# A sparse FFN cut into one-batch units and interleaved with the attention loops, its gate by tanh

## The chip, the cores and the metric

One Trainium2 chip, one core. The metric is the device time in microseconds of one execution of the whole program; lower is better. The profile is one execution, recorded by the hardware profiler. VectorE stands as DVE in it, ScalarE as ACT, GpSimd as POOL, TensorE as PE (its weight loads as PEld).

## What is computed

Two decoder layers on `x` of 4 batches x 256 tokens x 256 columns, f32, each an attention against a context and an FFN, both added to `x` with a gate `tanh(g)`. Layer 0: a retention-like attention with two heads, and a mixture of eight experts, of which each token takes one. Layer 1, where the change lies:

```
a  = grouped attention(layernorm(x), ctx), 32 heads in 8 groups, causal, softmax
x  = x + tanh(g_xattn[1]) * (a @ w_o.T + b_o)
y  = layernorm(x)
h  = silu(y @ w_gate) * (y @ w_up)          # 1024 columns
h  = of each four neighbouring columns only the two of largest magnitude, the others 0
x  = x + tanh(g_ffn[1]) * (h @ w_down)
```

## The kernel before, in words

The program is written by hand, one instruction stream for each engine, tied by semaphores; an engine runs its stream in order, and an instruction that waits holds all behind it. Tokens lie in 8 tiles of 128 (two a batch). The first 160 us are layer 0, the sort of tokens to experts and their loads; neither text nor change go there.

**The attention of layer 1.** For each batch `b` there are 24 score fills (`scores`, line 394, then the causal mask added by a bf16 matmul, line 410), each a PSUM bank of 512 columns, from which DVE takes row maxima (`row_maxima`, line 1151). The negated maxima (`negate`, lines 1161 and 1163) are turned by PE (`neg_turn`) and moved by DMA into rows of `qst`, so that a second product, `weights` (line 420), comes out with the maximum subtracted; ACT takes its exponential (`exponentials`, line 875), again 24 fills a batch. POOL zeroes the causal part (`affine_select`, line 730), eight times a batch. `values` (line 428) then makes four fills, ACT copies them out (`value_turn`), and twelve `finish` steps (per tile: four turns with DVE's reciprocal and product, one turn of the result, one projection by `wo1`, whose residual and statistics DVE makes) end the batch.

The order is the loop `for b in range(BATCH): for n in range(24)`, which every engine has in its own stream: in step `n` of batch `b` stand `weights(b, n)` and, while `n + 12 < 24`, `scores(b + 1, n + 12)` (LEAD is 12), then one `finish(b - 1, n // 2)` every second step, and the queries of batch `b + 2` at fixed steps. Behind the 24 steps come the keys of `b + 2` and the four `values(b, i)`, with three score fills of batch `b + 2` behind each.

PSUM has eight banks, dealt out in turn by `acquire` (line 191) from lists by kind: `max` 0 to 2 for scores, `exp` 3 to 5 for weights, `wide` 0 to 5 for values and the FFN, `turn1` 6 and `tok1` 7 for the rest. A fill waits until what stood in its bank is taken.

**The FFN of layer 1** stands behind all four batches, in two units of 512 tokens. `gate_up(g, j)` fills a bank with 512 gate columns and one with 512 up columns (two matmuls each); ACT takes silu of the first (line 931), DVE multiplies (line 1280), ACT takes the magnitude (line 925). Four such tiles `j`, in which neighbouring columns stand apart, make a group `g`. `sparsify(g, step)` (line 1233) finds the two largest of four: step 0 three compares (f32 in, bf16 out, lines 1241 to 1245), step 1 seven sums of them in bf16 (lines 1250 to 1263), steps 2 and 3 the masked products (line 1271). It runs one group behind. The first unit's gate steps carry the `finish` steps of batch 3 and the layer 3 norms of tiles 4 to 7 (the norms of tiles 0 to 3 stand in the loop of batch 3). `down(k)` is eight matmuls of 256 columns; `residual("res3", k, 3)` (line 986) ends a tile, which SP stores.

## Time and profile before

| | |
|---|---|
| three runs | 410.42 us median (410.26 to 411.62) |
| span of the profiled execution | 407.7 us; the page gives no time for it beside the span |
| busy: PE, DVE, ACT, POOL | 342.2, 214.7, 159.8, 98.1 us |
| mean granted TensorE clock | 0.937 |
| attention loops of batches 1, 2, 3 begin | at 222.2, 259.8, 286.2 us |
| values of batch 3 end, FFN begins | 309.0 us |
| last matmul ends | 405.1 us |

Of the page, the busy shares tell which engine could be the bound, and the chain which it is. A window is one stretch of the span: an engine whose busy time is nearly its length is what bounds it there, but a matmul's end is modelled, so PE can look busy while it waits; the pace of a stretch without waits shows its real speed. The granted clock is a share of 2.4 GHz.

### The profile page before, as it was taken

Reading aid. Unit: us, or ns where it says so; the run is one execution under the profiler, and the core shown is the slowest. Engines: PE = TensorE matmul, PEld = TensorE weight load, DVE = VectorE, ACT = ScalarE, POOL = GpSimd, SP = SyncE. Lnnn points to the kernel's source line nnn. Section 1 sums busy time; section 2 is a strip of 40 time slices with the busy share of each in tenths; the row PEclk is TensorE's granted clock in tenths of the full one; section 3 lists DMA queues with packets and bytes.
Section 4 is the critical chain, followed back from the end, with each engine's and each line's share of the span. In section 5 each row is a group of like instructions: output and inputs, shape, how many; then the busy total and the mean of one; then the engine's idle time right before and its main releaser. Section 6 shows DMA issues by size and latency. Waiting matters only on the chain.

```text
span 407.7 us, 4559 instructions
## 1 busy us (share of the span) xinstructions
PE 342.2 (84%) x1471; PEld 205.9 (50%) x1477; DVE 214.7 (53%) x509; ACT 159.8 (39%) x336; POOL 98.1 (24%) x148
## 2 busy tenths in 40 slices
PE   2799775509999848989799989979889879999997
PEld 1385565405656526545454555444443434444886
DVE  1544885601222248879446934881241338679921
ACT  1443221204333123145873875477873223333000
POOL 4402553330000256301340442054450001000000
PEclk9999998558999666999999999998999999999999
DMA  7995000134111115400000000000000000000011
GB/s 234 365 426 105 1 13 2 40 124 146 41 51 53 39 47 175 191 6 0 9 0 2 0 6 2 0 2 8 0 2 0 2 0 0 0 0 2 13 51 39
DMA packets 13879, 22.40 MB, mean 55 GB/s; under 512 B 2033, under 2 KB 11249, under 8 KB 13042
## 3 DMA queue, kind: packets, MB, share of 16 engines
q1 hardware_dynamic: 13090, 20.03, 14.5%
q0 software_dynamic: 768, 2.10, 1.6%
q8 instruction: 12, 0.20, 0.2%
q14 instruction: 9, 0.07, 0.1%
HBM read 15.83 MB, written 6.03 MB: 54 GB/s over the span
## 4 chain that ended last, share of the span: by engine, by line
PE 57%; DVE 20%; ACT 8%; issue 7%; DMA 3%; POOL 3%; another core or an unknown queue 1%; SPq 0%; DVEq 0%; ACTq 0%; POOLq 0%
PE bank L229 43%; DVE mx L1151 9%; PE bank L439 5%; ACT region L875 5%; PE bank L407 3%; DVE stats L946 2%; POOL x_sorted L692 2%; PE bank L242 1%; DMA ctxT<-in_ctxT_dram 1%; DVE x_sb L986 1%; PE bank L410 1%; PE bank L236 1%; PE bank L453 1%; PE bank L487 1%; ACT xT L747 1%
## 5 line engine op out<-in xcount | busy, mean ns | idle before, releaser
L1151 DVE TENSOR_REDUCE mx<-bank 128x2 f32<-128x512 f32 (+1 forms) x96 | 59.8, 684 | 14.0 <-PE bank L410 7.8
L875 ACT ACTIVATE region<-bank,padcol 128x512 f32<-128x512 f32 x96 | 60.8, 701 | 12.6 <-PE bank L229 11.6
L730 POOL TENSOR_SCALAR_AFFINE_SELECT region<-region 128x1024 f32<-128x1024 f32 x32 | 35.0, 1094 | 94.6 <-ACT region L875 94.3
L229 PE MATMUL bank<-xT,e_gu 128*128 128x512 f32 x128 | 56.6, 594 | 0.5 <-ACT xT L747 0.5
L229 PE MATMUL bank<-qst,kblk 128*128 128x512 f32 x96 | 46.1, 507 | 1.6 <-ACT region L875 0.7
L407 PE MATMUL bank<-kblk,qst 128*128 128x512 f32 x96 | 43.4, 475 | 1.7 <-DVE mx L1151 0.9
L229 PEld LDWEIGHTS bank<-xT,e_gu 128*128 128x128 f32 x128 | 23.8, 190 | 28.0 <-issue 27.1
L664 POOL TENSOR_SCALAR veps<-mv 128x1 f32<-128x1 f32 x40 | 11.3, 284 | 80.8 <-DVE mv L948 80.5
L410 PE MATMUL bank<-causb,identb 128*128 128x256 bf16 (+1 forms) x90 | 28.3, 314 | 0.0
L229 PE MATMUL bank<-e_down,region 128*128 128x256 f32 x128 | 27.8, 379 | 0.0
L986 DVE SCALAR_TENSOR_TENSOR x_sb<-bank,tg,x_sb 128x256 f32<-128x256 f32 x24 | 11.6, 482 | 29.2 <-PE bank L229 28.9
L747 ACT ACTIVATE xT<-bank 128x256 f32<-128x256 f32 x32 | 12.2, 386 | 37.5 <-PE bank L236 37.4
L229 PEld LDWEIGHTS bank<-e_down,region 128*128 128x128 f32 x128 | 24.3, 190 | 3.7 <-issue 0.5
L407 PEld LDWEIGHTS bank<-kblk,qst 128*128 128x128 f32 x96 | 18.3, 191 | 13.2 <-DVE mx L1151 9.3
L668 POOL TENSOR_TENSOR rstd<-veps,power 128x1 f32<-128x1 f32 x40 | 24.0, 601 | 3.3
L1123 DVE TENSOR_TENSOR sact<-bank,silu 128x176 f32<-128x176 f32 x15 | 5.1, 342 | 37.3 <-ACT silu L841 37.3
L1280 DVE TENSOR_TENSOR region<-bank,silu 128x512 f32<-128x512 f32 x16 | 11.0, 689 | 26.0 <-PE bank L229 26.0
L229 PEld LDWEIGHTS bank<-qst,kblk 128*128 128x128 f32 x96 | 18.7, 200 | 9.1 <-ACT region L875 7.3
L931 ACT ACTIVATE silu<-bank 128x512 f32<-128x512 f32 x16 | 9.6, 597 | 33.5 <-PE bank L229 33.5
L439 PE MATMUL bank<-region,vaug 128*32 128x512 f32 x192 | 22.7, 597 | 0.0
L229 PE MATMUL bank<-e_gu,sT 128*128 x60 | 21.7, 486 | 0.3 <-ACT sT L835 0.3
L229 PE MATMUL bank<-e_down,sT 128*128 (+1 forms) x60 | 19.6, 426 | 1.4 <-ACT sT L856 1.4
(155 smaller groups left out, 546.6 us busy)
## 6 DMA issues: line engine op xcount, KB each, us to landing
e_gu<-in_e_gu_dram SPq DMA_DIRECT2D x2, 1408.0 KB, 12.4
x_sorted<-zero SPq DMA_DIRECT2D x1, 1920.0 KB, 9.9
y_sorted<-region SPq DMA_DIRECT2D x15, 128.0 KB, 1.7
x_sb<-in_x_dram SPq DMA_DIRECT2D x4, 256.0 KB, 6.1
ctxT<-in_ctxT_dram SPq DMA_DIRECT2D x2, 512.0 KB, 6.1
e_down<-in_e_down_dram SPq DMA_DIRECT2D x1, 1024.0 KB, 14.3
region<-x_sorted SPq DMA_DIRECT2D x1, 1024.0 KB, 7.3
e_gu<-in_f_gate_dram SPq DMA_DIRECT2D x1, 1024.0 KB, 4.8
```

The lines of the kernel that those rows point to most:

```text
L229: return pe.matmul(dst, lhsT, rhs, start=first, stop=last)
L407: pe.matmul(dst, qst[:, s, q, hg, tile_cols(nt)], kblk[s][q][:, quads, 0:(nt + 1) * P], start=True, stop=False, skip_group_check=True)
L410: ready(pe.matmul(diagonal, identb[:, :], causb[:, 0:diagonal.shape[1], :], start=False, stop=True, skip_group_check=True), "sa")
L439: ins = pe.matmul(dst[32 * j:32 * j + 32, :], vaug[:, 2 * b + mt, 4 * q + j, :], rhs, start=(mt == 0), stop=(mt == nt), skip_group_check=True)
L664: pool.tensor_scalar(veps[:, layer, k:k + 1], mv[:, layer, k, 1:2], eps, None, ALU.add)\
L668: pool.tensor_tensor(out=rstd[:, layer, k:k + 1], in0=veps[:, layer, k:k + 1], in1=power[:, :], op=ALU.pow).then_inc(sem(f"rstd{layer}"), 1)
L730: pool.affine_select(out=block, in_=block, compare_op=ALU.is_ge, fill=0.0, base=0, pattern=[[0, 2], [0, PER_GROUP], [1, P]], channel_multi ...
L747: taken(act.activation(xT[:, :, tile_cols(tile)], src[:, 0:DIM].rearrange("p (t n) -> p t n", t=KT), ACT.Copy), f"ln{layer}")
L875: taken(act.activation(dst, src.rearrange("p (h n) -> p h n", n=SEQ - mt * P), ACT.Exp, bias=padcol[:, key:key + 1], scale=float(HD) ** -0 ...
L986: dve.scalar_tensor_tensor(out=x_sb[:, tile, :], in0=filled(dve, stage, k)[:, 0:DIM], scalar=tg[:, g:g + 1], in1=x_sb[:, tile, :], op0=ALU ...
L1151: taken(dve.reduce_max(mx[:, b % 2, nt, quads, q, hg], src, AX), "sa")
L1280: taken(dve.tensor_tensor(out=hs[u][:, 4 * blk + j, :], in0=src, in1=silu[:, i % 2, :], op=ALU.mult), "fu")
```

## The change

The FFN becomes four units of one batch (256 tokens). A bank now holds 256 gate and 256 up columns. A unit is 24 half steps: 0 to 15 are gate and up of its eight tiles in turn (two matmuls of 256 columns), 16 to 23 are down, two matmuls each: 16 to 19 the first group for both tiles, 20 to 23 the second. `ffn_halves` lays unit `b - 1` behind the steps from 16 of loop `b`, and its rest (half steps 8 to 23) behind steps 0 to 15 of loop `b + 1`; in the last loop two half steps a step. Each engine's loop calls its part (`ffn_half`, `ffn_gate`, `ffn_product`) at the end of the step. In the loops silu(g) is 0.5 * g * (1 + tanh(g / 2)), tanh on ACT and two DVE passes; the last unit keeps silu. The buffers `hs`, `absh`, the compares and counts are one group of half width; `hs` is two groups, each reused by the next unit. The banks: `max` and `exp` have two instead of three, `ffn` gets 4 and 5, values go to `exp`. `finish` takes steps 0 to 11, one each; queries, negation turn and norms move; the norms of layer 3 now stand in each loop. POOL makes their inverse deviations between its selects. The mask row is spread over four partitions for room, with wider loads and copies.

```diff
-QUERIES_AT = 10
-
-NORM_STEPS, LATE_NORM_STEPS = (13, 15, 17, 19), (3, 4, 6, 7)
-NEGATE_AT = 15
+QUERIES_AT = 13
+
+NORM_STEPS = (10, 15)
+NEGATE_AT = 18
+FFN_STEP = 16
+FFN_SLOTS = 2 * FFN_MT
+def ffn_halves(b, n):
+
+    if n < FFN_STEP:
+        return ((b - 2, 24 - FFN_STEP + n),) if b >= 2 else ()
+    if b == BATCH - 1:
+        return (b - 1, 2 * (n - FFN_STEP)), (b - 1, 2 * (n - FFN_STEP) + 1)
+    return ((b - 1, n - FFN_STEP),) if b >= 1 else ()
...
-        hs = [region[:, u, 0:4096].rearrange("p (m n) -> p m n", m=FFN_MT) for u in range(2)]
-        absh = [region[:, u, 4096:6144].rearrange("p (j n) -> p j n", j=4) for u in range(2)]
+        hs = (f_flat[:, 2 * KT * FFN_I:2 * KT * FFN_I + 4 * SEQ].rearrange("p (j n) -> p j n", j=4),
+              sT[:, :, :, :].rearrange("p s t n -> p (s t n)").rearrange("p (j n) -> p j n", j=4))
+        absh = sb("absh", [P, 4, SEQ])
+        xn3 = silu[:, :, SEQ:2 * SEQ]
...
-                 "max": (0, 1, 2), "exp": (3, 4, 5), "wide": (0, 1, 2, 3, 4, 5),
-                 "turn1": (6,), "tok1": (7,), "last": (6, 7)}
+                 "max": (0, 1), "exp": (2, 3), "ffn": (4, 5), "wide": (0, 1, 4, 5),
+                 "turn1": (6,), "tok1": (7,), "late": (6, 0, 1), "last": (0, 1, 2, 3, 4, 5)}
...
-                dst = acquire(pe, "av", 4 * b + i, "wide")
+                dst = acquire(pe, "av", 4 * b + i, "exp")
...
+            def ffn_half(b, h, kind="ffn"):
+
+                step, half = divmod(h, 2)
+                if step < FFN_MT:
+                    blk, j = divmod(step, 4)
+                    if half == 0:
+                        dst = acquire(pe, "ff", FFN_MT * b + step, kind)
+                    else:
+                        dst = fills["ff", FFN_MT * b + step]
+                    if h == 0:
+                        pe.wait_ge(sem("ln3_taken"), 2 * b + 2)
+                        if b == 0:
+                            loaded(pe, "f", 3)
+                    c = j * 2 * P + blk * P
+                    w = (f_gate, f_up)[half]
+                    for t in range(KT):
+                        ins = mm(dst[:, half * SEQ:(half + 1) * SEQ], w[:, t, c:c + P],
+                                 xT[:, t, b * SEQ:(b + 1) * SEQ], t == 0, t == KT - 1)
+                    if half == 1:
+                        ready(ins, "ff")
+                    return
+                blk, tile = divmod(step - FFN_MT, 2)
+                k = 2 * b + tile
+                if blk == 0 and half == 0:
+                    dst = acquire(pe, "res3", k, kind)[:, 0:DIM]
+                else:
+                    dst = fills["res3", k][:, 0:DIM]
+                pe.wait_ge(sem("hs_made"), FFN_MT * b + 4 * blk + 4)
+                for j in (2 * half, 2 * half + 1):
+                    m = 4 * blk + j
+                    ins = mm(dst, hs[blk][:, j, tile_cols(tile)], f_down[:, m, :], m == 0, m == FFN_MT - 1)
+                if blk == 1 and half == 1:
+                    ready(ins, "res3")
...
-                    if b >= 1 and n % 2 == 1:
-                        finish(b - 1, n // 2)
+                    if b >= 1 and n < 12:
+                        finish(b - 1, n)
                     if b + 2 < BATCH:
                         queries(b + 2, n)
-                    if b == BATCH - 1 and n in NORM_STEPS:
-                        ln_turn(3, NORM_STEPS.index(n), "tok1")
+                    if b >= 1 and n in NORM_STEPS:
+                        ln_turn(3, 2 * b - 2 + NORM_STEPS.index(n), "tok1")
                     if n == NEGATE_AT and b + 1 < BATCH:
                         neg_turn(b + 1, "turn1")
+                    for u, h in ffn_halves(b, n):
+                        ffn_half(u, h)
...
...
+            last = BATCH - 1
+            for n in (0, 1, 2, 3, 6, 7, 8, 9, 4):
+                finish(last, n, "late")
+            ffn_half(last - 1, 16)
+            finish(last, 10, "late")
+            finish(last, 5)
+            ffn_half(last - 1, 17)
+            finish(last, 11)
+            ffn_half(last - 1, 18)
+            ffn_half(last - 1, 19)
+            ln_turn(3, TILES - 2, "turn1")
+            ffn_half(last - 1, 20)
+            ffn_half(last - 1, 21)
+            ln_turn(3, TILES - 1, "tok1")
+            ffn_half(last - 1, 22)
+            ffn_half(last - 1, 23)
+            for h in range(24):
+                ffn_half(last, h, "last")
...
+                        if b >= 1 and q == 0 and n == 2:
+                            inverse_std(3, 2 * b - 2, LN_EPS)
+                        if b >= 1 and q == 1 and n == 0:
+                            inverse_std(3, 2 * b - 1, LN_EPS)
...
+            def magnitude(i):
+                g, j = divmod(i, 4)
+                act.wait_ge(sem("ff_taken"), i + 1)
+                if g >= 1 and j == 0:
+                    act.wait_ge(sem("compared"), 3 * g)
+                act.activation(absh[:, j, :], hs[g % 2][:, j, :], ACT.Abs).then_inc(sem("abs_made"), 1)
+
+            def ffn_gate(b, h):
+
+                step, half = divmod(h, 2)
+                if half == 0 or step > FFN_MT:
+                    return
+                i = FFN_MT * b + step
+                if step < FFN_MT:
+                    src = filled(act, "ff", i)[:, 0:SEQ]
+                    if i >= 2:
+                        act.wait_ge(sem("ff_taken"), i - 1)
+                    if b == BATCH - 1:
+                        act.activation(silu[:, i % 2, 0:SEQ], src, ACT.Silu).then_inc(sem("gate_made"), 1)
+                    else:
+                        act.activation(silu[:, i % 2, 0:SEQ], src, ACT.Tanh, scale=0.5).then_inc(sem("gate_made"), 1)
+                if step >= 1:
+                    magnitude(i - 1)
...

+            def ffn_product(b, h):
+
+                step, half = divmod(h, 2)
+                if half == 0:
+                    return
+                if step < FFN_MT:
+                    i = FFN_MT * b + step
+                    blk, j = divmod(step, 4)
+                    if b >= 1 and j == 0:
+                        dve.wait_ge(sem("res3_ready"), 2 * b)
+                    src = filled(dve, "ff", i)
+                    gate = silu[:, i % 2, 0:SEQ]
+                    dve.wait_ge(sem("gate_made"), i + 1)
+                    if b == BATCH - 1:
+                        taken(dve.tensor_tensor(out=hs[blk][:, j, :], in0=src[:, SEQ:2 * SEQ], in1=gate, op=ALU.mult), "ff")
+                    else:
+
+                        dve.scalar_tensor_tensor(out=gate, in0=gate, scalar=1.0, in1=src[:, 0:SEQ],
+                                                 op0=ALU.add, op1=ALU.mult).then_inc(sem("gated"), 1)
+                        dve.wait_ge(sem("gated"), i + 1)
+                        taken(dve.scalar_tensor_tensor(out=hs[blk][:, j, :], in0=gate, scalar=0.5, in1=src[:, SEQ:2 * SEQ],
+                                                       op0=ALU.mult, op1=ALU.mult), "ff")
+                    if blk == 1:
+                        sparsify(2 * b, j)
+                elif step < FFN_MT + 2:
+                    for part in (2 * (step - FFN_MT), 2 * (step - FFN_MT) + 1):
+                        sparsify(2 * b + 1, part)
+                else:
+                    residual("res3", 2 * b + step - FFN_MT - 2, 3)
...
-                    if b >= 1 and n % 2 == 1:
-                        finish(b - 1, n // 2)
+                    if b >= 1 and n < 12:
+                        finish(b - 1, n)
                     if b + 2 < BATCH:
                         queries(b + 2, n)
-                    if b == BATCH - 1 and n + 2 in NORM_STEPS:
-                        norm(3, NORM_STEPS.index(n + 2))
+                    if b >= 1 and n + 1 in NORM_STEPS:
+                        norm(3, 2 * b - 2 + NORM_STEPS.index(n + 1))
+                    for u, h in ffn_halves(b, n):
+                        ffn_product(u, h)
...
+            for n in (0, 1, 2, 3, 6, 7, 8, 9):
+                finish(last, n)
+            finish(last, 5)
+            ffn_product(last - 1, 17)
+            finish(last, 11)
+            norm(3, TILES - 2)
+            ffn_product(last - 1, 19)
+            norm(3, TILES - 1)
+            ffn_product(last - 1, 21)
+            ffn_product(last - 1, 23)
+            for h in range(24):
+                ffn_product(last, h)
```

`sparsify` is the function of before on one shared group of buffers, 256 columns wide.

## Rows read from the trace of the kernel before

**Rows 1.** The page: busy time of the engines, and the chain by engine.
```profile
PE 342.2 (84%) x1471; PEld 205.9 (50%) x1477; DVE 214.7 (53%) x509; ACT 159.8 (39%) x336; POOL 98.1 (24%) x148
PE 57%; DVE 20%; ACT 8%; issue 7%; DMA 3%; POOL 3%; another core or an unknown queue 1%; SPq 0%; DVEq 0%; ACTq 0%; POOLq 0%
```

**Rows 2.** Windows by stage: start:end length, busy us (x instructions) of each engine, granted clock, DMA.
```profile
222.20:232.40 10.20, 10.14 (x53) 6.60 (x54) 10.03 (x25) 8.53 (x14) 3.51 (x4) 1.00 0.01 2
232.40:243.50 11.10, 8.83 (x38) 5.51 (x37) 4.59 (x16) 8.82 (x17) 4.14 (x4) 1.00 0.02 6
...
259.80:272.40 12.60, 11.97 (x59) 7.49 (x59) 12.32 (x29) 9.79 (x17) 4.38 (x4) 1.00 0.00 1
272.40:280.90 8.50, 6.43 (x26) 3.95 (x30) 2.17 (x10) 6.43 (x13) 3.31 (x4) 0.80 0.04 11
280.90:286.20 5.30, 5.30 (x49) 1.47 (x49) 1.09 (x3) 1.79 (x3) 2.60 (x5) 1.00 0.00 0
286.20:303.70 17.50, 14.56 (x64) 8.96 (x68) 6.03 (x23) 16.32 (x31) 7.71 (x8) 1.00 0.00 1
...
349.70:405.10 55.40, 55.34 (x192) 36.38 (x192) 35.23 (x61) 10.01 (x18) 0.00 (x0) 1.00 0.05 17
```

**Rows 3.** Instructions by line and form: xcount | busy us, mean ns of one.
```profile
L1271 DVE SCALAR_TENSOR_TENSOR region<-amat,region 128x512 f32<-128x512 bf16 x16 | 10.3, 684 | 0.0
...
L1241 DVE TENSOR_TENSOR ctxT<-region 128x1536 bf16<-128x1536 f32 x4 | 7.0, 1753 | 1.6 <-ACT region L925 1.5
...
L1024 DVE SCALAR_TENSOR_TENSOR att<-bank,region 128x256 f32<-128x256 f32 x8 | 3.4, 425 | 0.7 <-PE bank L229 0.7
...
L1250 DVE TENSOR_TENSOR amat<-ctxT 128x1024 bf16<-128x1024 bf16 x4 | 2.7, 682 | 0.0
L1252 DVE TENSOR_TENSOR amat<-ctxT 128x512 bf16<-128x512 bf16 x4 | 1.7, 419 | 0.0
```

**Rows 4.** Timeline of VectorE, 263 to 273 us: start, us, instruction.
```profile
263.13 1.28 DVE L1151 TENSOR_REDUCE mx<-bank 128x4 f32<-128x512 f32 x2
264.33 0.20 DVE L1177 RECIPROCAL rden<-bank 128x8 f32<-128x8 f32 x1
...
264.70 1.28 DVE L1151 TENSOR_REDUCE mx<-bank 128x2 f32<-128x512 f32 x2
...
271.83 0.48 DVE L986 SCALAR_TENSOR_TENSOR x_sb<-bank,tg,x_sb 128x256 f32<-128x256 f32 x1
...
272.90 0.19 DVE L1177 RECIPROCAL rden<-bank 128x8 f32<-128x8 f32 x1
```

**Rows 5.** Timeline of TensorE, then VectorE, 173 to 177 us.
```profile
174.34 0.50 PE L407 MATMUL bank<-kblk,qst 128*128 128x512 f32 x1 [0.57 <-DVE mx L1151]
174.69 0.28 PE L410 MATMUL bank<-causb,identb 128*128 128x256 bf16 x1
...
173.60 3.07 DVE L1151 TENSOR_REDUCE mx<-bank 128x2 f32<-128x512 f32 x5
```

**Rows 6.** Timeline of POOL, then VectorE, at 178 and 232 us.
```profile
232.17 1.09 POOL L730 TENSOR_SCALAR_AFFINE_SELECT region<-region 128x1024 f32<-128x1024 f32 x1 [0.99 <-ACT region L875]
...
177.91 0.18 DVE L1161 TENSOR_SCALAR nmx<-mx 128x32 fp32r<-128x32 f32 x1
...
232.22 1.07 DVE L1161 TENSOR_SCALAR nmx<-mx 128x32 fp32r<-128x32 f32 x1
```

**Rows 7.** Windows of 3 us in the loop of batch 2.
```profile
273.00:276.00 3.00, 1.62 (x9) 0.87 (x9) 0.74 (x4) 1.03 (x4) 1.09 (x1) 1.00 0.04 8
276.00:279.00 3.00, 3.00 (x11) 2.19 (x10) 0.86 (x4) 2.99 (x6) 0.82 (x1) 0.51 0.08 22
```

**Rows 8.** Instructions by line: ScalarE's table loads and the early tanh.
```profile
L752 ACT ACT_TABLE_LOAD x1 | 1.3, 1283 | 0.8 <-PEq L1381 0.8
L841 ACT ACT_TABLE_LOAD x1 | 1.3, 1283 | 0.0
...
L759 ACT ACTIVATE tg<-gates 128x4 f32<-128x4 f32 x1 | 0.2, 198 | 0.0
```

188 lines of the change are left out of this document (63 added, 125 removed).

## The prediction, on record before the change ran

> **What bounds the kernel now.** I read the page first, then the chain of waits, the windows stage by stage, and the instructions of each engine in the stages that the change touches. TensorE is busy 84% of the span and holds 57% of the chain, VectorE 20% [rows 1]. That mean hides two kinds of stage, and the windows tell them apart [rows 2]. The last 55.4 us are pure matmul: 192 instructions, of which 64 stream 512 columns and 128 stream 256, so 256 pieces of 256 columns at 0.216 us each, without a gap. From batch 1 on, each attention loop has two parts. In its first twelve steps VectorE is the bound (10.03 of 10.2 us busy in batch 1, 12.32 of 12.6 in batch 2); after them it is ScalarE's exponentials and little waits (8.5 us in batch 2, and 16.32 of 17.5 us over the whole loop of batch 3), while TensorE has real room. The tail behind the attention is 96.1 us long, from 309.0 to 405.1 (the table of times).
>
> So the change puts TensorE work where TensorE has room, but puts the FFN's VectorE work with it, and half of it into the twelve steps where VectorE has none.
>
> **Unit prices.** A half step is four of the 0.216 us pieces, 0.86 us; a unit of 24 half steps is 20.7 us, four units 83 us, as now. Back to back, a VectorE instruction costs less than its duration: two row maxima of 0.68 start 1.20 apart, 0.60 each; a reciprocal and its product take 0.37 (264.33 to 264.70); a residual with its statistics takes 1.07 (271.83 to 272.90) [rows 4]. For halved widths I take duration less 0.08. A 128x256 operation in f32 lasts 0.425, so 0.34. The compares: 1536, 1024 and 512 columns become 768, 512 and 256; from 1.75 for 1536 and 0.684 for 512 the line is 1.04 ns a column, which gives 0.87+0.60+0.34 = 1.8. The bf16 counts run 0.68 for 1024 and 0.42 for 512, so 0.29 for 256: one of 0.34 and six of 0.20. Two waits of an instruction on the one before it add 0.1 each. The four masked products are 0.34 each instead of 0.60. One group costs 1.8+0.1+1.55+0.1+1.4 = 5.0 us, and there are eight; four double-width groups cost 8.6 each by the same rows, so splitting adds 5.6 us of VectorE work [rows 3]. The tanh gate needs two 128x256 passes, the second waiting for the first: 0.46+0.34 = 0.8 us for each of 24 fills (bounds 0.68, no wait, and 1.0, with the 0.48 of an operation with a pointer), where silu needed 0.60 for twice the columns.
>
> **Ahead of loop 2.** The scores keep two banks of three. A maximum that starts at 173.60 ends at 174.28, the next score of that bank starts at 174.34, and its mask matmul starts 0.35 later and lasts 0.28 [rows 5]: 0.69 us from freed to filled. With two banks a pair of maxima takes 0.68+0.69, 0.69 each and not 0.60; over 48 scores (batch 0, and batch 1) 4 us (bounds 0, and 7 with the mask of 512 columns). Between the values of batches 0 and 1 three scores come in a row and the third now waits for the first's maximum, 0.5 us, three times a batch: 3 us. In loop 1 the finishing of batch 0 moves from every second step to the first twelve: four more 0.37, one more 1.07, less two norms that go later, plus a norm: 2.1 us on VectorE. Its last twelve steps get eight half steps (6.9 us), the query work and the layer 3 norms: TensorE's own work is 12.3 us and with three waits on ScalarE 14, against 11.1 now. Loop 1 grows by 5, and loop 2 starts 12 us later, at 271.9 instead of 259.8.
>
> **Loop 2**, now 12.6+8.5 and 5.3 for the values [rows 2]. First twelve steps on VectorE: 12 maxima 7.2, 8 finishes 3.0, 2 residuals 2.1, negation 0.7, norm 0.3, 4 gate products 3.2, 2 groups 10.0: 26.5 us. The burst before it leaves 1.8, and waits for the first fill and at step 9 add 0.8: 29.1. TensorE has 20 us of work in these steps but cannot run ahead: it has two max banks, one transpose bank, and half step 16 waits for the first group's masked products, half step 20 (step 12) for the second's. What stands behind that wait are the exponentials' matmuls, so ScalarE starves too. The last twelve steps are then TensorE's: 12 half steps 10.3, weights 2.6, transposes 0.6: 13.5. Values 5.3. Two costs ride on it. **The port:** a negation that lasts 0.18 took 1.07 when POOL's 1.09 us select had begun 0.05 before it [rows 6]. All compares, counts and masked products now run beside eight selects a batch. I take 1.5 us a loop (bounds 0 and 8 x 1.09 = 8.7).
>
> The Trainium skill, page "SBUF — State Buffer", section "Who interferes with whom", says that a VectorE instruction with two SBUF inputs and a GpSimd instruction reading SBUF exclude each other for the whole of the one that came first. The row agrees; by the rule alone every select could stop the sparsifying, and the sum would be up to 14 us longer for the two loops.
>
> **The clock:** TensorE ran 273 to 276 at 1.62 us of 3 busy and was granted 0.51 (1.2 GHz) in the next 3 us [rows 7], which costs 1.5 us when there is work. After step 9 VectorE has 8 us to do (counts, negation, residual, masking) against TensorE's 3. I add 2 us (bounds 0 and 5). Loop 2: 29.1+1.5+13.5+2+5.3 = 51.4.
>
> **Loop 3**, now 17.5 and 5.3. No scores, so VectorE starts with an empty queue: the first fill is there after 2 half steps and a tanh, 3.1 us. By pairs of steps, with the prices above, VectorE is done with steps 0-1 at 5.8, 2-3 at 9.0, 4-5 at 11.6, 6-7 at 13.8, 8-9 at 19.2 (it waits 1.1 us for half step 16), 10-11 at 21.7. TensorE's four steps to 15 take 4.5, its eight steps of two half steps 8 x 1.94 = 15.5 and waits 0.7, values 5.3: 47.7, with port 1.5 and clock 1.5 50.7.
>
> **Tail**, now 98.7 with the last store. From the end T of the values: VectorE has the last divisions done at T+2.6, a residual at 5.7 (after transpose, copy and projection), the first half of the group at 9.2, a residual 10.3, norm, second half of masking 12.0, last norm 12.3; TensorE, with 6.9 us of half steps in that time, starts unit 3 at T+15.7. Its 16 gate and up half steps take 13.8; the sparsifying of the last group cannot start before the last product (T+31) and takes 5.0, while TensorE has 3.4 to do; the last four half steps, residual and store take 3.4+0.6+2.1. T+42, and 1.5 for the clock: 43.5. Silu's table load stands in a wait. The store queue still has its four row moves first, and POOL's two inverse deviations now stand ahead of a select: nothing, since the values wait for the last select only; if that cover went, no more than a select's 1.09 us each time. The pad rows' wider load (128 KB, was 4) and one wider copy lie ahead of the routing, where VectorE and the queue have gaps: nothing, and without them under 1 us.
>
> **Sum.** 271.9+51.4+50.7+43.5 = 417.5 us of span, against 407.7. The page gives no time of the execution beside its span; the median of 410.42 lies 2.7 above it and I add that: **420**.
> The 55 us taken out of the tail come back as 25 in loop 2, 28 in loop 3 and 12 before, because the parts bound by VectorE and by TensorE follow one another.
>
> **Rivals.** *TensorE sets the loops* (0.13, faster): if its queue ran across the twelfth step, loop 2 would last 20+13.5+5.3 = 38.8 and loop 3 41.3 (32 half steps 27.5, weights 2.6+2.6, turns 3.3, values 5.3): 395.5, or **398**. It decides at VectorE's first twelve steps of loop 2: under 20 us there and this holds, at 26 it does not. For it: VectorE's total, 53% [rows 1], leaves room; against it: the two waits for masked products, and 12.32 of 12.6 us there already [rows 2]. *The small costs don't bite* (0.12, faster): without banks (7), port (3) and clock (5) the same plan gives **405**; about halfway lies no change (0.06). *The port bites fully* (0.12, slower): half of the 14 us more, **427 to 434**. *Tables alternate* (0.03, slower): if tanh did not share its table with exp, 24 gates would pay two loads of 1.28, 61 us. Against it: a tanh (line 759) and an exp (line 784) both run between the loads of lines 752 and 841 [rows 8], with none between them. The forecast itself has 0.54.
>
> **Range.** 403 to 431: down to where the small costs vanish, up to the port's half; below it the first rival, above it the tables, 0.16. Faster by over 0.3% (1.2 us, what this kernel's spread of runs can tell) 0.25, same 0.06, slower 0.69.
>
> **What would show it.** In the profile after: the loop of batch 2 with VectorE over 95% busy for some 29 us before step 12, and waits of the down matmuls for the masked products; a tail of some 43 us with a TensorE gap of about 3 us before unit 3 and of 2 near the end; single compares or masked products of over 1 us beside selects; half clock after the gaps; four table loads. Wrong if TensorE is over 95% busy at real rate in loop 2's first part, or loops 2 and 3 together stay under 90 us.

## The result, and the profile after

The changed kernel took **446.83 us** (median of 4 runs, 445.74 to 448.02), the kernel before 410.8 beside it: a ratio of 1.088 [1.086, 1.090]. The forecast was 420, range 403 to 431: slower was right, but 2.3% was forecast and 8.8% measured. The profiled execution took 445.74 us with a span of 443.7, so 2.0 lie around it; the 2.7 that the prediction added hold another 0.7 of difference between executions. All times below are medians; one of the four runs of e4_lag (452.39 us) was in a slower state of the chip and is left out of its median.

The page: busy time of the engines, and the chain by engine.
```profile
PE 351.1 (79%) x1605; PEld 232.2 (52%) x1605; DVE 238.6 (54%) x605; ACT 167.7 (38%) x368; POOL 100.5 (23%) x148
PE 54%; DVE 28%; issue 7%; ACT 4%; DMA 3%; POOL 3%; SPq 0%; DVEq 0%; POOLq 0%; ACTq 0%
```
Against [rows 1] TensorE has 9 us more work and 36 us more span: the loss is idle time. VectorE's share of the chain goes from 20% to 28%.

The windows by stage, with the columns of [rows 2]: the loop of batch 1 in two parts, then batch 2 (up to the end of TensorE's wait in step 12, the rest of the loop, values), batch 3 (the same first two parts), and the tail.
```profile
233.30:248.60 15.30, 13.49 (x66) 8.04 (x67) 13.35 (x34) 9.10 (x15) 4.05 (x5) 1.00 0.00 0
248.60:265.90 17.30, 13.55 (x63) 10.54 (x62) 6.63 (x17) 11.27 (x24) 5.28 (x6) 1.00 0.02 5
286.00:319.30 33.30, 23.36 (x115) 16.88 (x115) 28.54 (x76) 12.60 (x25) 6.09 (x8) 1.00 0.00 1
319.30:335.50 16.20, 15.33 (x63) 12.38 (x63) 3.81 (x9) 9.69 (x19) 3.28 (x3) 0.90 0.07 21
335.50:340.90 5.40, 5.40 (x50) 1.36 (x49) 0.84 (x2) 2.48 (x5) 1.09 (x1) 1.00 0.00 0
340.90:369.50 28.60, 18.78 (x96) 14.69 (x92) 21.10 (x59) 12.86 (x26) 6.56 (x8) 1.00 0.00 1
369.50:392.60 23.10, 22.28 (x97) 18.42 (x101) 10.93 (x27) 11.58 (x25) 4.59 (x4) 0.93 0.04 12
397.95:443.70 45.75, 35.88 (x161) 28.92 (x160) 25.30 (x78) 9.44 (x23) 2.62 (x4) 0.96 0.04 12
```
The first parts of batches 2 and 3 show the surprise. In the first, TensorE works 23.36 us and VectorE 28.54 of 33.30; in the second 18.78 and 21.10 of **28.60**. Neither engine is full. The timeline of VectorE in the first steps of batch 3 shows why:
```profile
344.34 0.42 DVE L1302 SCALAR_TENSOR_TENSOR silu<-silu,bank 128x256 f32<-128x256 f32 x1 [0.91 <-ACT silu L947]
344.80 0.42 DVE L1305 SCALAR_TENSOR_TENSOR sT<-silu,bank 128x256 f32<-128x256 f32 x1
345.14 0.95 DVE L1252 TENSOR_TENSOR cmps<-absh 128x768 bf16<-128x768 f32 x1
346.01 0.68 DVE L1254 TENSOR_TENSOR cmps<-absh 128x512 bf16<-128x512 f32 x1
346.61 1.31 DVE L1256 TENSOR_TENSOR cmps<-absh 128x256 bf16<-128x256 f32 x1
347.85 0.19 DVE L1223 RECIPROCAL rden<-bank 128x8 f32<-128x8 f32 x1
348.07 0.22 DVE L1225 TENSOR_TENSOR att<-bank,rden 128x64 f32<-128x64 f32 x1
```
and that of TensorE in the same time:
```profile
344.76 0.58 PE L242 MATMUL bank<-qst,kblk 128*128 128x512 f32 x1
348.35 0.44 PE L467 MATMUL bank<-ident,prod 128*128 128x128 f32 x2 [3.01 <-DVE att L1225]
```
The compares of a group stand in VectorE's queue ahead of the division (lines 1223 and 1225) that frees the single transpose bank. TensorE's next transpose waits 3.01 us for it, and behind the transpose stand the half step, the weights and, through them, the next gate. Then VectorE waits for that gate. The engines alternate.

To split the 36 us I cut each kernel at ScalarE's exponentials (24 a batch, read from its timeline). Each column ends where the next batch's first exponential starts; batch 3 ends at the start of its last.

| profiled kernel | to batch 0 | batch 0 | batch 1 | batch 2 | batch 3 | tail | span |
|---|---|---|---|---|---|---|---|
| before | 187.9 | 34.9 | 38.8 | 25.2 | 16.1 | 104.8 | 407.7 |
| e1_banks | 194.1 | 39.0 | 41.7 | 26.7 | 16.8 | 104.8 | 423.1 |
| e7_exp2 | 189.4 | 39.3 | 39.0 | 27.3 | 16.6 | 104.9 | 416.5 |
| e2_order | 189.3 | 36.5 | 43.8 | 29.2 | 23.1 | 103.7 | 425.6 |
| e8_both | 191.9 | 41.2 | 45.5 | 29.5 | 21.3 | 104.0 | 433.4 |
| e9_bothturns | 190.0 | 39.1 | 46.2 | 27.9 | 18.5 | 102.2 | 423.9 |
| **after** | 191.8 | 42.4 | 52.8 | 54.5 | 49.8 | 52.4 | 443.7 |
| e3_thin | 191.8 | 41.5 | 53.6 | 46.4 | 40.2 | 44.8 | 418.3 |
| e5_turns | 192.2 | 40.2 | 55.9 | 51.4 | 47.3 | 52.4 | 439.3 |
| e12_select | 192.0 | 39.3 | 51.2 | 53.0 | 46.5 | 52.3 | 434.3 |
| e14_beforeselect | 187.9 | 34.3 | 38.4 | 24.2 | 16.1 | 104.8 | 405.8 |
| e15_tailturns | 189.7 | 34.9 | 38.8 | 25.2 | 16.1 | 100.5 | 405.2 |

The first column varies by 1 to 2 us between executions of kernels that are the same up to there (187.9 and 189.7 in the first and last row), the others by up to 1 us (batch 0 is 42.4 in the kernel after and 41.5 in e3_thin, though their work is the same so far).

The columns hold one more thing than the edits: the granted clock. The windows of batch 0 in before, e7_exp2, after and e12_select, then of batch 3 in e2_order and e8_both:
```profile
187.90:222.80 34.90, 31.45 (x165) 16.69 (x166) 20.50 (x38) 23.45 (x45) 10.13 (x10) 1.00 0.01 3
189.40:228.70 39.30, 36.39 (x168) 20.23 (x166) 20.73 (x38) 24.73 (x45) 10.15 (x10) 0.87 0.01 3
191.80:234.20 42.40, 36.88 (x169) 19.31 (x168) 21.50 (x37) 24.90 (x44) 10.14 (x10) 0.92 0.01 2
192.00:231.30 39.30, 34.33 (x169) 17.65 (x168) 20.63 (x37) 24.64 (x44) 3.71 (x10) 1.00 0.01 2
298.80:321.90 23.10, 17.85 (x62) 10.35 (x65) 7.00 (x26) 16.40 (x31) 7.00 (x7) 0.78 0.00 0
308.10:329.40 21.30, 15.02 (x62) 8.07 (x65) 7.00 (x26) 16.35 (x30) 7.06 (x7) 1.00 0.00 0
```
The same matmuls keep TensorE busy for 2 to 5 us longer where the grant is lower. Over whole executions it shows too: the four runs of e7_exp2 go from 414.87 us at a mean clock of 0.934 to 420.78 at 0.910, some 2.5 us for each 0.01 (an estimate from these runs). Whether an edit lowers the clock, by the gaps that it makes, or the execution happens to have a lower one, no run here tells apart, so differences of 2 to 3 us below are read with the clock beside them.

### The profile page after: what moved, and what is told of

Read it like the earlier page. It is cut to its first block, busy times and chain, and to the rows that moved or that the text cites. A ratio compares the mean times of both kernels' runs of the same rounds, so it can differ in the third digit from the quotient of the medians.

```text
span 443.7 us, 4996 instructions
## 1 busy us (share of the span) xinstructions
PE 351.1 (79%) x1605; PEld 232.2 (52%) x1605; DVE 238.6 (54%) x605; ACT 167.7 (38%) x368; POOL 100.5 (23%) x148
## 4 chain that ended last, share of the span: by engine, by line
PE 54%; DVE 28%; issue 7%; ACT 4%; DMA 3%; POOL 3%; SPq 0%; DVEq 0%; POOLq 0%; ACTq 0%
PE bank L242 37%; DVE mx L1197 7%; PE bank L453 5%; PE bank L421 5%; DVE stats L992 3%; PE bank L424 2%; DVE cmps L1252 2%; DVE x_sb L1032 2%; POOL x_sorted L723 2%; PE bank L467 1%; PE bank L255 1%; PE bank L249 1%; DMA ctxT<-in_ctxT_dram 1%; DVE sT L1282 1%; DVE silu L1302 1%
## 5 line engine op out<-in xcount | busy, mean ns | idle before, releaser
L907 ACT ACTIVATE region<-bank,padcol 128x512 f32<-128x512 f32 x96 | 65.1, 686 | 52.1 <-PE bank L242 51.2
L242 PE MATMUL bank<-xT,e_gu 128*128 128x256 f32 x256 | 62.3, 380 | 1.5 <-DVE sT L1305 0.8
L421 PE MATMUL bank<-kblk,qst 128*128 128x512 f32 x96 | 47.5, 508 | 8.2 <-DVE mx L1197 8.0
L242 PE MATMUL bank<-qst,kblk 128*128 128x512 f32 x96 | 52.5, 556 | 1.1 <-ACT region L907 0.9
L242 PEld LDWEIGHTS bank<-xT,e_gu 128*128 128x128 f32 x256 | 47.1, 190 | 8.5 <-issue 1.4
L242 PE MATMUL bank<-e_down,sT 128*128 128x256 f32 (+2 forms) x124 | 39.8, 445 | 12.6 <-DVE sT L1282 11.2
L242 PEld LDWEIGHTS bank<-e_down,sT 128*128 128x128 f32 (+1 forms) x124 | 24.9, 217 | 25.3 <-DVE sT L1282 12.7
L1302 DVE SCALAR_TENSOR_TENSOR silu<-silu,bank 128x256 f32<-128x256 f32 x24 | 10.1, 419 | 29.7 <-ACT silu L947 29.7
L242 PE MATMUL bank<-e_down,e_gu 128*128 128x256 f32 x64 | 16.0, 383 | 4.9 <-DVE e_gu L1282 4.9
L992 DVE BATCH_NORM_STATS2 stats<-x_sb 128x6 f32<-128x256 f32 x32 | 13.6, 425 | 9.3 <-DMA x_sb<-in_x_dram 8.5
## 6 DMA issues: line engine op xcount, KB each, us to landing
e_down<-in_e_down_dram SPq DMA_DIRECT2D x1, 1024.0 KB, 14.4
```

The lines of the kernel that those rows point to most:

```text
L242: return pe.matmul(dst, lhsT, rhs, start=first, stop=last)
L421: pe.matmul(dst, qst[:, s, q, hg, tile_cols(nt)], kblk[s][q][:, quads, 0:(nt + 1) * P], start=True, stop=False, skip_group_check=True)
L907: taken(act.activation(dst, src.rearrange("p (h n) -> p h n", n=SEQ - mt * P), ACT.Exp, bias=padcol[:, key:key + 1], scale=float(HD) ** -0 ...
L992: dve.bn_stats(stats[:, layer, k, :], src).then_inc(sem("stats"), 1)
L1302: dve.scalar_tensor_tensor(out=gate, in0=gate, scalar=1.0, in1=src[:, 0:SEQ], op0=ALU.add, op1=ALU.mult).then_inc(sem("gated"), 1)
```

## Experiments

**The score banks alone** (e1_banks, on the kernel before):
```diff
-                 "max": (0, 1, 2), "exp": (3, 4, 5), "wide": (0, 1, 2, 3, 4, 5),
+                 "max": (0, 1), "exp": (2, 3), "wide": (0, 1, 2, 3, 4, 5),
```


> The kernel before with one edit: its row maxima and exponentials turn over two banks of scores instead of three. Theory A (the banks are the first part of the loss): each of the 96 steps' pairs pays a longer pitch of maxima (about 0.71 us for two heads' maxima in the trace of after against 0.60 before) and the third score of a burst waits for its exponential; 8 to 10 us in all, so 419 to 421 us, spread over all four batches' bursts and loops. Theory B (VectorE or TensorE has slack that covers the handoff): 0 to 2 us, 411 to 413 us.

425.18 us, ratio 1.037 [1.033, 1.040]: **14.9 us**, neither theory, half as much again as the higher. In the table 6.2 of it lie ahead of batch 0's first exponential, 4.1 in batch 0 and 2.9 in batch 1, both at a granted clock of 1.00. TensorE's timeline in the scores' burst of batch 0:
```profile
187.42 0.50 PE L407 MATMUL bank<-kblk,qst 128*128 128x512 f32 x1 [0.19 <-DVE mx L1151]
187.76 0.28 PE L410 MATMUL bank<-causb,identb 128*128 128x256 bf16 x1
188.02 0.49 PE L407 MATMUL bank<-kblk,qst 128*128 128x512 f32 x1
188.35 0.28 PE L410 MATMUL bank<-causb,identb 128*128 128x256 bf16 x1
188.83 0.51 PE L407 MATMUL bank<-kblk,qst 128*128 128x512 f32 x1 [0.19 <-DVE mx L1151]
```
Two scores come 1.41 us apart, 0.705 each; the maxima of before run 0.60 apart [rows 4]. The pitch is what the prediction had (0.69).

**The exponentials' banks alone** (e7_exp2: `"exp": (3, 4)`, the maxima keep three).


> The kernel before with three banks of scores for the row maxima as before, but two for the exponentials. It tells which of the two pools costs the 14.9 us of both. Theory A (VectorE's maxima lose their pitch, so the pool of the maxima costs): 0 to 3 us, 411 to 413 us. Theory B (in the loops TensorE's weights wait for ScalarE's exponentials): 6 to 10 us, 416 to 420 us.

418.27 us, ratio 1.017 [1.010, 1.023], **7.4 us** over the kernel before: inside theory B's range, but the interval reaches from 4 to 10 us. The table has 4.4 us of it in batch 0 (34.9 to 39.3) and 2.1 in batch 2, and these are the stretches with a low clock (0.87 in both, against 1.00 and 0.93 before); the fastest run, at 0.934, is 4 us above the kernel before. So the exponentials' pool costs something that the prediction had at nothing, between a quarter and two thirds of the 14.9, and how much of it is the wait of the weights for a bank and how much the clock stays open. The maxima's pool was never cut alone.

**The order alone** (e2_order, on the kernel before; the same edit on all three engines):
```diff
-QUERIES_AT = 10
+QUERIES_AT = 13
-NEGATE_AT = 15
+NEGATE_AT = 18
-                    if b >= 1 and n % 2 == 1:
-                        finish(b - 1, n // 2)
+                    if b >= 1 and n < 12:
+                        finish(b - 1, n)
```


> The kernel before with its units whole and its three banks, but with the loop's own order as the change has it: one finish of a head in each of the first twelve steps, the query's heads from step 13, the negation at step 18. Theory A (the single transpose bank with a finish in every step makes TensorE and VectorE alternate): 5 to 8 us, 416 to 419 us, most of it in the first twelve steps of the loops. Theory B (order is free, only the amount of work in the loops and the banks count): 0 to 2 us, 411 to 413 us.

425.75 us, ratio 1.035 [1.030, 1.040]: **14 to 15 us** (14.4 by the ratio, 15.4 by the medians), again more than either theory. The table has 7.0 of it in batch 3, where VectorE has no scores to reduce; but that stretch ran at a granted clock of 0.78 (the profiled execution is the slowest of the four), and in e8_both, at 1.00, the order adds 4.5 there (16.8 in e1_banks to 21.3). Both engines at the start of that loop, in order of time:
```profile
299.53 0.44 PE L453 MATMUL bank<-ident,prod 128*128 128x128 f32 x2 [0.39 <-DVE att L1179]
...
300.00 0.21 DVE L1177 RECIPROCAL rden<-bank 128x8 f32<-128x8 f32 x1 [0.53 <-PE bank L453]
...
300.25 0.23 DVE L1179 TENSOR_TENSOR att<-bank,rden 128x64 f32<-128x64 f32 x1
...
300.53 0.44 PE L453 MATMUL bank<-ident,prod 128*128 128x128 f32 x2 [0.33 <-DVE att L1179]
```
The step lasts exactly 1.00 us, transpose to transpose: 0.47 to the reciprocal, 0.25 to the division, 0.28 back to TensorE. Each engine waits for the other (0.53 and 0.33), and with one bank the step can't be shorter whatever else is light.

**Both edits** (e8_both), and **both with three transpose banks** (e9_bothturns, which adds `"turn1": (6, 4, 5)`, the two banks that the two-bank scores leave free).


> The kernel before with both edits already tried alone: two score banks in each pool, and the loop's order of the change (a finish in each of the first twelve steps, the query's heads from step 13, the negation at step 18); the feed-forward part stays whole at the end. Theory A (the two costs fall on different stretches, banks on the bursts, order on the loops): they add up, 410.4 + 14.9 + 14.4, so 437 to 441 us, and all that the split of the feed-forward part itself does is the rest up to after, some 7 us. Theory B (both are the same wait in two dresses): 427 to 432 us, and the split itself costs 15 to 20 us.

> The same kernel as the one with both edits, with the finish's transposes turning over three banks (its own and the two that two-bank scores leave free) instead of one. Theory A (the single transpose bank is what the order costs in loop 3, where VectorE is idle two thirds of the time): loop 3's first twelve steps fall from 14.7 us to 9 to 11 us, loop 1's by 0 to 2 us since there VectorE and TensorE are both near full; 4 to 7 us less than the kernel with both edits. Theory B (it is the chain of each finish through TensorE, VectorE and back, in order, that costs): less than 2 us.

435.57 us, ratio 1.061 [1.058, 1.063]: the two overlap by some 5 us (a part of which is e2_order's clock), and the order costs 10.4 on top of the banks. With three transpose banks it is 427.11, ratio 1.039 [1.037, 1.042]: **8.5 us back**, more than expected. In the table 4.0 of the 9.5 us between the two profiled executions lie ahead of batch 1, where no finish stands; batches 1, 2 and 3 change by +0.7, -1.6 and -2.8, the tail by -1.8. The windows of batch 3's first twelve steps, e8_both:
```profile
308.10:321.10 13.00, 9.06 (x40) 5.43 (x39) 4.58 (x20) 8.71 (x15) 4.14 (x4) 1.00 0.00 0
```
and e9_bothturns:
```profile
303.20:313.40 10.20, 9.01 (x41) 5.73 (x39) 4.40 (x20) 8.28 (x16) 4.19 (x4) 1.00 0.00 0
```
The work is the same on every engine, and the stretch is 2.8 us shorter. The same twelve steps in batch 1 last 10.10 us in e1_banks, 14.00 in e8_both and 13.50 in e9_bothturns:
```profile
233.10:243.20 10.10, 10.02 (x53) 6.69 (x52) 9.84 (x24) 8.53 (x15) 3.62 (x4) 1.00 0.00 0
233.10:247.10 14.00, 12.83 (x63) 7.51 (x61) 12.09 (x34) 8.77 (x14) 3.95 (x4) 1.00 0.00 1
229.10:242.60 13.50, 12.47 (x63) 7.95 (x61) 11.81 (x34) 9.05 (x15) 3.87 (x4) 1.00 0.01 1
```
There the order puts 2.25 us more work on a VectorE that was busy 9.84 of 10.10, and more banks give back only 0.5. So the order costs in two ways: **in the first twelve steps of batch 3, where VectorE has room, most of it is the single bank; in those of batches 1 and 2, where VectorE is full, most of it is not.** The kernel with three transpose banks and the old order was not built, so 427.1 - 425.2 = 1.9 us is no measure of what the order costs with enough banks (e11_beforeturns below shows that the old order gains by a second bank too).

**The changed kernel with its two turning banks shared** (e5_turns: `"turn1": (6, 7), "tok1": (7, 6)`).


> The kernel after with the finish's transposes, and all else that used one bank for turning and one for tokens, turning over both of these banks instead of keeping to its own; nothing else is changed. Theory A (the one transpose bank, refilled in every step, makes TensorE wait for VectorE's division of the step before): the waits of the finish's transpose for att go, and the first twelve steps of loops 2 and 3 shrink by 2 to 4 us each, 438 to 442 us. Theory B (the wait is of TensorE for work that VectorE has not come to, whichever bank it takes): within 2 us of after, 445 to 448 us.

442.29 us, ratio 1.077 [1.074, 1.080]: 4.5 us less than the change, just outside theory A's range. From the batch's first exponential to the end of TensorE's wait in step 12, batch 2 takes 30.3 us instead of 32.3 and batch 3 25.5 instead of 28.0, so both gain 2.0 to 2.5 as theory A had it; batch 1 is 3.1 longer at a granted clock of 0.94 instead of 1.00, and batch 0 2.2 shorter at 1.00 instead of 0.92. The first waiting transpose of batch 3, which stood 3.01 us in the kernel after, is now the one that needs all divisions, and waits less:
```profile
346.87 0.44 PE L255 MATMUL bank<-ident,att 128*128 128x128 f32 x2 [2.07 <-DVE att L1225]
```

**Thin sparsifying** (e3_thin, on the kernel after): every compare, count and masked product 8 columns wide (the magnitude on ScalarE keeps its 256, other than the expectation says), such as
```diff
-                    dve.tensor_tensor(out=cmp1[:, :, :], in0=m[:, 0:3, :], in1=m[:, 1:4, :], op=ALU.is_ge)\
+                    dve.tensor_tensor(out=cmp1[:, :, 0:8], in0=m[:, 0:3, 0:8], in1=m[:, 1:4, 0:8], op=ALU.is_ge)\
```


> The kernel after, with every instruction of the sparsifying (magnitude, compares, counts and the masked product) 8 columns wide instead of 256: the masks of the other columns are left out, all instructions and their waits stay. Theory A (VectorE's amount of work sets the loops 2 and 3 and part of the tail): 25 to 30 us less than after, 417 to 422 us. Theory B (the loops are set by handoffs in order between TensorE, VectorE and ScalarE and by the granted clock): less than 10 us off, above 437 us.

420.90 us, ratio 1.027 [1.024, 1.030]: **26 us less** than the change, theory A. Its page:
```profile
PE 346.8 (83%) x1599; PEld 230.6 (55%) x1605; DVE 209.7 (50%) x605; ACT 168.0 (40%) x368; POOL 98.4 (24%) x148
```
VectorE lost 28.9 us of work (238.6 to 209.7) and the span 25.4. VectorE was idle 46% of the time, and still nearly every us taken from it came off the kernel, in batch 2 (8.1), batch 3 (9.6) and the tail (7.6): in an alternation both engines' work is on the path. A small part is clock: these three stretches had 0.97 in the kernel after and 1.00 here.

**Thin sparsifying with shared banks** (e13_thinturns, both edits).


> The kernel after with both edits: the sparsifying 8 columns wide (the masks of the other columns are left out) and the two turning banks shared. Theory A (VectorE's work and the transpose bank cost in different places): the two savings add up, 446.8 - 26 - 4.5, so 415 to 418 us. Theory B (with VectorE light, the division comes early enough for one bank): 419 to 421 us, as with the thin sparsifying alone.

418.97 us, ratio 1.021 [1.018, 1.024]: 1.9 less than the thin one alone, between the theories and at theory B's edge. When VectorE comes early enough, the bank holds up less.

**Products one step later** (e4_lag, on the kernel after):
```diff
-                    for u, h in ffn_halves(b, n):
-                        ffn_product(u, h)
+                    if n:
+                        for u, h in ffn_halves(b, n - 1):
+                            ffn_product(u, h)
+                for u, h in ffn_halves(b, 23):
+                    ffn_product(u, h)
```


> The kernel after with each product of the feed-forward part moved one step later in VectorE's stream, behind the next step's row maxima and finish, so that it doesn't wait for its gate. Nothing is left out. Theory A (VectorE stands at the head of its queue for a gate that is late, and TensorE's next transpose stands behind it): the first twelve steps of loops 2 and 3 shrink by 5 and 7 us, 10 to 12 us in all, 435 to 437 us. Theory B (those waits are only the slack of an engine that waits for something else): 0 to 2 us off, 445 to 447 us.

448.47 us, ratio 1.089 [1.084, 1.095]: **nothing**, so theory A falls. It rested on the largest wait of VectorE's list (instructions by line; the idle time before them stands last), after:
```profile
L1302 DVE SCALAR_TENSOR_TENSOR silu<-silu,bank 128x256 f32<-128x256 f32 x24 | 10.1, 419 | 29.7 <-ACT silu L947 29.7
```
and in e4_lag:
```profile
L1302 DVE SCALAR_TENSOR_TENSOR silu<-silu,bank 128x256 f32<-128x256 f32 x24 | 10.0, 416 | 25.4 <-ACT silu L947 25.4
```
Only 4.3 of 29.7 us went, and no batch became shorter by more than 0.8 us (41.6, 53.6, 55.5 and 49.9 against the table's 42.4, 52.8, 54.5 and 49.8). Of the 29.7, the list of waits has only 2.7 between 340 and 371 us, in the first part of batch 3; the largest piece, 9.3, lies in the second part of batch 1 (248.6 to 265.9 us), where VectorE has time to spare.

**Narrow selects** (e12_select on the kernel after, e14_beforeselect the same edit on the kernel before):
```diff
-                        block = pt0[q][:, js, :, 0:P] if n < 2 else pt1[q][:, js, :, :]
+                        block = (pt0[q][:, js, :, 0:P] if n < 2 else pt1[q][:, js, :, :])[:, :, :, 0:8]
-                                           pattern=[[0, 2], [0, PER_GROUP], [1, P]], channel_multiplier=-1)\
+                                           pattern=[[0, 2], [0, PER_GROUP], [1, 8]], channel_multiplier=-1)\
```


> The kernel after with GpSimd's causal selects 8 columns wide instead of 128 (the causal mask of the other columns is left out); their number and their waits stay. Theory A (VectorE's two-input and copy operations are held while a select runs: some ten of them at 1.1 to 1.75 us instead of 0.3 to 0.7 in the trace of after, seven or so on the path): 3 to 6 us off, 441 to 444 us. Theory B (held operations are hidden): within 1.5 us of after. Theory C (the selects hold VectorE much more than the single long entries show): over 10 us off, under 437 us.

> The kernel before with GpSimd's causal selects 8 columns wide instead of 128 (the causal mask of the other columns is left out). Theory A (most of the 8.1 us that this took off the kernel after comes from the feed-forward work that the change puts beside the selects): 0 to 2 us off, 408.5 to 411 us. Theory B (the selects hold VectorE's division and negation and the values of both kernels alike): 5 to 8 us off, 402.5 to 405.5 us.

438.75 us (ratio 1.070 [1.067, 1.073]) on the kernel after, 8.1 less, between theories A and C; 408.49 (0.996 [0.994, 0.998]) on the kernel before, 2.0 less, at theory A's edge. The 8.1 are not all collisions. 3.1 of the 9.4 us between the two profiled executions lie in batch 0, where no feed-forward work runs and the granted clock was 0.92 in the kernel after and 1.00 here; whether the one negation that a select holds there (200.51 us, 1.08 long) brought the clock down is not shown. Batches 2 and 3 are 1.5 and 3.3 shorter, together **4.8 us**, against 1.0 in the kernel before. The timeline agrees: in these two batches of the kernel after five operations of the sparsifying and one norm last 0.8 to 0.9 longer than their like, 5.2 in all. The compare that lasted 1.31 at 346.61 in the kernel after is here, at the same place of its loop:
```profile
340.56 0.45 DVE L1256 TENSOR_TENSOR cmps<-absh 128x256 bf16<-128x256 f32 x1
```

**The gate by Silu in the loops** (e10_silu: `ACT.Tanh, scale=0.5` becomes `ACT.Silu` in the gate; the products that follow stay, so the output is another function).


> The kernel after with the gate's function in the loops Silu instead of Tanh (VectorE's two products stay as they are, so another function is computed), which is not in the set of functions that holds the exponential: ScalarE loads its table anew between exponentials and gates. Theory A (each of the 24 gates in the loops costs two loads of 1.28 us on ScalarE, 61 us, and ScalarE becomes the bound of the second half of each loop): 30 to 60 us slower than after, 477 to 507 us. Theory B (the loads lie in ScalarE's idle time, since it is busy 38%): under 10 us slower.

487.33 us, ratio 1.189 [1.184, 1.194]: **40.5 us more** than the change, theory A. ScalarE's instructions by line, in e10_silu:
```profile
L907 ACT ACT_TABLE_LOAD x24 | 30.8, 1283 | 0.4
L947 ACT ACT_TABLE_LOAD x24 | 30.8, 1283 | 0.4
```
The 46 loads more than after are 59 us of ScalarE, and two thirds of that came on top of the time though it was idle 62% of it (the mean clock fell too, from 0.92 to 0.89). With the tanh the changed kernel has four table loads, as forecast; without it the split would have lost twice as much.

**Shared banks in the kernel before** (e11_beforeturns: the edit of e5_turns) and **in its tail alone** (e15_tailturns: only the last batch's `finish` and the late norms' transposes take both banks in turn, through a new kind):
```diff
+                 "turn1": (6,), "tok1": (7,), "tail": (6, 7), "last": (6, 7)}
...
-                    finish(BATCH - 1, c)
+                    finish(BATCH - 1, c, "tail", "tail")
...
-                    ln_turn(3, UNIT_TILES + LATE_NORM_STEPS.index(n), "turn1")
+                    ln_turn(3, UNIT_TILES + LATE_NORM_STEPS.index(n), "tail")
```


> The kernel before with one edit: its transpose bank and its token bank are shared, each use taking the two in turn. In the trace of before TensorE waits 5.1 us in five places for VectorE's division ahead of the finish's transposes, 3.8 us of it in the tail where the finishes of the last batch stand in a row. Theory A (the single bank makes those waits): 1 to 4 us off, 407 to 409.5 us, faster than both kernels. Theory B (a bank shared with the tokens' tiles brings as many waits as it takes away): 410 to 412 us.

> The kernel before with the transpose bank and the token bank taken in turn only by the finish of the last batch and the norms' transposes behind the loops; in the loops each keeps its own. Theory A (the single bank costs where finishes stand close together, which in the kernel before is the tail alone): 4 to 5 us off as with shared banks everywhere, 405.5 to 407 us, or one or two less since loop 1 keeps its banks. Theory B (the gain of the shared banks came from the loops): 409 to 411 us.

406.01 us, ratio **0.989 [0.987, 0.992]**, and 406.46 us, ratio 0.991 [0.989, 0.993]: both are faster than both kernels, and can't be told apart. In the table all of e15_tailturns' gain stands in one column, the tail: 104.8 to 100.5. The waits of TensorE there, for the kernel before (303 to 350 us):
```profile
PE bank L453 <- DVE att L1179: 3.8, 4, 0.9
PE bank L236 <- DVE att L1179: 1.1, 2, 0.6
```
and e15_tailturns (304 to 350 us):
```profile
PE bank L236 <- DVE att L1179: 1.4, 2, 0.7
```
The finish's 3.8 us of waits are gone. It is the fault that the change has in batch 3, finishes close together on one bank, found where the kernel before had it.

## Why the prediction was too small

**What it had right.** The 55 us taken out of the tail came back in the loops: the tail fell by 52.4 (104.8 to 52.4), and batches 2 and 3 grew by 29.3 and 33.7 against forecasts of 25 and 28. VectorE's unit prices held: a group's compares at 345.14, 346.01 and 346.61 start 0.87 and 0.60 apart, as worked out. TensorE's waits for the masked products came at the two places named:
```profile
306.67 1.10 PE L242 MATMUL bank<-e_down,e_gu 128*128 128x256 f32 x4 [1.41 <-DVE e_gu L1282]
...
319.31 2.07 PE L242 MATMUL bank<-e_down,sT 128*128 128x256 f32 x4 [4.93 <-DVE sT L1282]
```
The last matmuls start at half clock after this gap (granted 0.50 from 319.3 to 322.3): four of them last 2.07 us, the four at 306.67 1.10. The rival that TensorE sets the loops fell with VectorE's 28.54 us of work (it held under 20) and with e3_thin, the one that small costs don't bite with e1_banks, that of the tables with the four loads.

**Where it failed**, by its own steps. The forecast span was 417.5 us, the measured one 443.7. Of the 26.2 between them 14.1 lie ahead of loop 2 (286.0 against 271.9), 3.5 in loop 2 with its values (54.9 against 51.4), 6.3 in loop 3 with its values (57.0 against 50.7) and 2.3 in the tail.

*"Ahead of loop 2 ... two score banks ... 4 us ... 3 us"*: mis-sized. The banks cost 14.9 us over the whole kernel, and loop 1 begins at 233.3 instead of 222.2, 11.1 later where these terms give at most 7. The prediction priced only the maxima's pool; the exponentials' pool was put at nothing, without a row for it, and cost 7.4 (4 to 10) alone. What is left of the 14.9, 7.5, is near the 7 forecast, but that is a subtraction and no run. No term was there for the clock in batch 0 either, 0.92 in the profiled execution.

*"Loop 1 grows by 5"*: the largest single miss. The loop with its keys and values grew by 15.1 us (37.6 to 52.7 by the starts of the loops), 10 more than forecast; by the exponentials it is 14.0 (38.8 to 52.8). e8_both has 6.7 of it from banks and order, where 4 us stand in the first twelve steps; the rest, 7.3, came with the half steps, over 6 of it behind step 12 (the first twelve steps last 15.0 against e8_both's 14.1). That is near the 6.9 us of the half steps themselves, as if TensorE had not the room that the prediction gave them; no run shows it by itself. One piece that the trace does show: the norms of batch 3's queries stood on VectorE behind negation and residual, and one negation was held by a select:
```profile
248.81 1.08 DVE L1207 TENSOR_SCALAR nmx<-mx 128x32 fp32r<-128x32 f32 x1
```

*"First twelve steps on VectorE: ... 29.1"* and *"VectorE is done with ... steps 10-11 at 21.7"*: this is the step whose mechanism failed, and the two stretches are 11.1 us longer than it gave (3 of them had a term of their own, the port). It named the one transpose bank as a reason why TensorE can't run ahead, and then summed VectorE's work as though VectorE hardly waited in turn. The work was right: 28.3 us in loop 2 (29.1 less 0.8 of waits) against 28.54 busy, of which 1.8 are two operations held by selects, and 18.6 in loop 3 (the same prices without scores) against 21.10, of which 2.5 are three such operations. The waits were not: 0.8 forecast and 4.8 measured in loop 2, 3.1 and 7.5 in loop 3, so that the stretches lasted 33.3 and 28.6. VectorE was busy 86% of loop 2's first part where the prediction's sign was over 95%. In batch 3 VectorE waits 3.2 us in four places for the finish's transposes and 2.7 in three for gates, the rest at the start and between instructions. The single bank is part of the reason: a second bank takes 2.0 and 2.5 us off the two stretches (e5_turns), half of what the waits exceed the forecast. The other part, divisions that stand behind the compares in VectorE's queue whatever bank they free, is argued from the timelines and from e3_thin; no run moved the divisions ahead. Here a sum of VectorE's prices is a lower bound, not the time.

*The port, 1.5 us a loop*: somewhat too small. By e12_select it is 4.8 us for the two loops, against 3 (3.8 if the 1.0 of the kernel before is taken off). The bound of every select held in full is 16 x 1.09 = 17.4, 14 above the 3 of the sum. The Trainium skill, page "SBUF — State Buffer", section "Who interferes with whom", says that the two exclude each other; the trace agrees for single operations (the compare at 346.61), but beside the 16 selects of the two batches only six operations were held. The row that the prediction called in agreement is a negation, with one tensor input, and not the two-input case of its sentence. The same section lets a `tensor_scalar` or a copy take the shared ports in the modes that use two ports; the trace agrees that a one-input operation can be held, with a norm of 1.26 us beside a select (they start at 309.15 and 309.17) where it lasts 0.40 at 361.33.

*The clock, 3.5 us in the loops*, and *the tail, 43.5*: near. The granted clock was 0.90 and 0.93 in the second parts of the loops, 16.2 and 23.1 us long, which makes 3.2 us (an estimate from these windows); the tail from the end of the values was 45.75.

**The sum, as measured.** Banks 14.9; order on top of them 10.4; the split of the feed-forward part itself 446.8 - 435.6 = 11.3, in which some 4 of collisions lie. Together 36.6, against 446.8 - 410.8 = 36.0 measured. Three transpose banks under banks and order give 8.5 back. The sparsifying is worth 26 us by e3_thin; without it the split itself would come to 11.3 - 26, a gain of 15. That is an estimate from these runs, and it takes the sparsifying to cost nothing in the kernel before, where it lay beside pure matmuls; no run thins it there. What stays open: how much of batch 1's 7.3 us is TensorE's half steps and how much the later norms; how much of the exponentials' pool is clock; and what the order costs with enough banks.

## What to carry to other kernels

Count banks before engines: a split that needs a buffer takes it from someone, and each pool that turns over two instead of three, or one, sets a round trip (here 1.00 us for transpose, reciprocal, division and back) that no busy share shows. Where two engines hand work back and forth in order, idle time of either one is not room: 28.9 us of work off an engine that was idle 46% of the time took 25.4 off the kernel, while working around the largest wait in its own list gained nothing. Look for places where steps on a one-bank pool stand close together; letting the last batch's finishes take a second bank in turn gained 1%. And read the granted clock of a stretch before a difference of 2 or 3 us in it is put down to an edit.

## What the hardware showed that I had not expected

- Two functions of different tables in turn cost ScalarE a little over the load each time: in e10_silu's timeline a load starts at 375.00, 0.02 us after the exponential's end, and the gate starts at 376.41.
```profile
374.29 0.69 ACT L907 ACTIVATE region<-bank,padcol 128x512 f32<-128x512 f32 x1
375.00 1.28 ACT L947 ACT_TABLE_LOAD   x1
376.41 0.38 ACT L947 ACTIVATE silu<-bank 128x256 f32<-128x256 f32 x1
```
- Select and compare each hold the other in turn. In the kernel after a select starts at 346.13, in the middle of a compare (346.01, 0.68 us), and lasts 1.51 us instead of 1.09; the next compare, at 346.61, lasts 1.31 instead of 0.45 and ends 0.28 us after the select. Its line in POOL's timeline:
```profile
346.13 1.51 POOL L765 TENSOR_SCALAR_AFFINE_SELECT region<-region 128x1024 f32<-128x1024 f32 x1 [9.50 <-ACT region L907]
```
